# Wavelet convolution with a split-precision pyramid: level 3 in paired matmuls, up-sampling with stacked halves

## What is computed

```python
def _L1_conv_ref(x, base_w, base_b, base_scale, wconv_w, wscale):
    cur = x
    for i in range(3):                                 # three Haar levels
        co = haar2d(cur)                               # 2x2 blocks -> ll, lh, hl, hh
        cur = co[:, :, 0]
        flat = dwconv(co.reshape(B, C * 4, h, w), wconv_w[i]) * wscale[i]   # 5x5, per channel
        level_coeffs.append(flat.reshape(B, C, 4, h, w))
    next_ll = 0
    for i in reversed(range(3)):
        co = level_coeffs[i].at[:, :, 0].add(next_ll)
        next_ll = ihaar2d(co)                          # back to twice the size
    return dwconv(x, base_w) * base_scale + base_b + next_ll

x = x + _L0_conv_ref(_gn(x), ...)
x = x + _L1_conv_ref(_gn(x), ...)
```

## Time and profile before

| | us |
|---|---|
| median of 3 runs | 11311.51 (11306.57 to 11315.59) |
| the profiled execution | 11311.75 |
| its span | 11309.9 |
| PE / DVE / ACT / POOL busy | 10853.3 / 9314.2 / 6979.7 / 3419.9 |

### The profile page before, as it was taken

One profiled execution on the slowest core, in us unless ns is written; L12 is line 12 of the kernel. 1 busy time (PEld: TensorE's weight loads), 2 busy tenths in 40 slices (PEclk: granted clock), 3 DMA queues, 4 the chain that ended last, 5 costly groups with the idle time before them and its releaser, 6 DMA issues.

```text
span 11309.9 us, 208798 instructions
## 1 busy us (share of the span) xinstructions
PE 10853.3 (96%) x68772; PEld 9284.1 (82%) x68772; DVE 9314.2 (82%) x16092; ACT 6979.7 (62%) x11660; POOL 3419.9 (30%) x2756
## 2 busy tenths in 40 slices
PE   4999999999999999999599999999999999999999
PEld 4888888888888888888588888888888888888888
DVE  6989999899998989988677777777777777777777
ACT  4777777777777777788445445454454545545454
POOL 3444444344444444444222122212222122221221
PEclk9999999999999999999799999999999999999999
DMA  5333233233333333222266666666666766667665
GB/s 184 126 101 125 96 123 123 92 129 101 114 114 116 113 101 130 93 80 81 73 140 151 148 148 147 145 153 147 149 145 145 154 146 150 144 146 153 145 150 118
DMA packets 1149039, 1453.41 MB, mean 129 GB/s; under 512 B 201567, under 2 KB 1111199, under 8 KB 1111455
## 3 DMA queue, kind: packets, MB, share of 16 engines
q1 hardware_dynamic: 1147231, 1442.74, 50.1%
q10 hardware_dynamic: 1376, 6.13, 0.1%
HBM read 1040.06 MB, written 408.56 MB: 128 GB/s over the span
## 4 chain that ended last, share of the span: by engine, by line
PE 49%; DVE 1%; SPq 0%; DMA 0%; issue 0%; POOL 0%; DVEq 0%; POOLq 0%
PE ps_w L1274 10%; PE ps_w L1275 10%; PE ps_w L1276 10%; PE ps_ll L1282 4%; PE ps L1274 4%; PE ps L1275 4%; PE ps L1276 4%; PE ps_w L1317 4%; DVE ob L1399 0%; DVE x L1337 0%; DMA yb<-y_scratch 0%; SPq L1101 0%; SPq L1110 0%; DMA prm<-params 0%; SPq L1120 0%
## 5 line engine op out<-in xcount | busy, mean ns | idle before, releaser
L1274 PE MATMUL ps_w<-zb,mat 128*128 128x512 f32 x4800 | 1925.7, 401 | 1.6 <-DVE ob L1399 1.6
L1276 PE MATMUL ps_w<-zb,mat 128*128 128x512 f32 x4800 | 1907.6, 397 | 0.0
L1275 PE MATMUL ps_w<-zb,mat 128*128 128x512 f32 x4800 | 1907.2, 397 | 0.0
L1227 ACT ACTIVATE z<-x,prm 64x384 f32<-64x384 f32 (+1 forms) x3072 | 1807.2, 659 | 55.5 <-DVE x L1337 47.8
L635 POOL CAST xn_hi<-xs 96x512 fp32r<-96x512 f32 x1024 | 842.7, 823 | 3106.9 <-PE ps_qkv L660 2255.4
L1173 POOL CAST mat<-raw 128x1280 fp32r<-128x1280 f32 (+1 forms) x288 | 344.8, 1215 | 4454.8 <-DMA raw<-vec 2674.2
L1399 DVE SCALAR_TENSOR_TENSOR ob<-ps_w,prm,x 64x512 f32<-64x512 f32 x1920 | 1440.6, 750 | 148.7 <-PE ps_w L1317 109.5
L1337 DVE SCALAR_TENSOR_TENSOR x<-yb,prm,xb 128x1024 f32<-128x1024 f32 (+1 forms) x576 | 1120.4, 1997 | 421.6 <-DMA prm<-params 374.9
L658 PE MATMUL ps_qkv<-wqkv_hi,xn_hi 96*128 96x288 f32 x4096 | 1388.4, 339 | 38.0 <-POOL xn_lo L637 19.8
L637 POOL TENSOR_TENSOR xn_lo<-xs,xn_hi 96x512 fp32r<-96x512 f32 x1024 | 1363.7, 1332 | 81.9
L1247 ACT ACTIVATE ll<-ps_ll 128x512 f32<-128x512 f32 x192 | 115.1, 599 | 1880.5 <-PE ps_ll L1282 1880.5
(11 more groups left out here) (183 smaller groups left out, 24815.2 us busy)
## 6 DMA issues: line engine op xcount, KB each, us to landing
xst<-in_x SPq DMA_DIRECT2D x96, 2048.0 KB, 13.8
xs<-in_x SPq DMA_DIRECT2D x128, 1536.0 KB, 8.9
y_scratch<-ys SPq DMA_DIRECT2D x128, 1536.0 KB, 9.5
out<-ob SPq DMA_DIRECT2D x768, 208.0 KB
xb<-in_x SPq DMA_DIRECT2D x576, 256.0 KB
yb<-y_scratch SPq DMA_DIRECT2D x576, 256.0 KB
raw<-vec SPq DMA_DIRECT2D x192, 320.0 KB, 5.4
raw<-vec SPq DMA_DIRECT2D x384, 160.0 KB, 4.2
```

The source lines that it names most:

```text
L1227: last = nc.scalar.activation(z[q * WROWS:(q + 1) * WROWS, ts, b, :], x1[slot(k, g)][rows, pairs, b, q::2], ACT.Identity, scale=prm[k][row ...
L1274: mm(out_, w[HI], xx[HI], start=start, stop=False)
L1275: mm(out_, w[HI], xx[LO], start=False, stop=False)
L1276: return mm(out_, w[LO], xx[HI], start=False, stop=stop)
```

## The change

Level 3: the high and low parts of its input lie in one tile `in3_hl`, so that one matmul of 256 columns multiplies the high matrix with both; its results for high and low stand side by side in `ps_3`, and the product of the low matrix with the high input (128 columns) is added onto the first. ACT copies all of `ps_3` to `s3`, and DVE adds the two halves there (`sum3`) before `up_levels` goes on.

Up-sampling: rows 0 to 63 and 64 to 127 of `next_ll` are split apart. `next_a` holds the high part of the upper 64 rows on partitions 0 to 63 and their low part on 64 to 127; `next_b` the same for the lower rows. The matrices `up_sb` hold each half twice, one above the other, so one matmul adds high and low. Windows 0 and 1 need only the upper rows, windows 3 and 4 only the lower, window 2 both.

Of the diff only renames, sizes of tiles and the three small tensors that change their allocation are left out.

```diff
@@ ACT, steps @@
                     act.wait_ge(l3_ready, qn + 1)
-                    nc.scalar.activation(s3[:], ps_3[:, 0, 0:IMGS * HALF // 4], ACT.Copy).then_inc(s3_copied, 1)
+                    nc.scalar.activation(s3[:].rearrange("p s h n -> p (s h n)"), ps_3[:].rearrange("p s n -> p (s n)"),
+                                         ACT.Copy).then_inc(s3_copied, 1)
                     act.wait_ge(next_ready, qn + 1)
-                    nc.scalar.activation(next_p[HI][:], next_ll[:].rearrange("p n c -> p (n c)"), ACT.Copy
-                                         ).then_inc(next_hi, 1)
+                    both = next_ll[:].rearrange("p n c -> p (n c)")
+                    nc.scalar.activation(next_a[0:64, :], both[0:64], ACT.Copy).then_inc(next_hi, 1)
+                    nc.scalar.activation(next_b[64:128, :], both[64:128], ACT.Copy).then_inc(next_hi, 1)
@@ PE, steps @@
-                    level(ps_3, mat3, in3_p, HALF // 4).then_inc(l3_ready, 1)
+                    for s in range(2):
+                        for d in range(TAPS):
+                            both = (ps_3[:, s, :], mat3[HI][:, s, d, :], in3_hl[:, :, s, :, d:d + HALF // 4])
+                            high = (ps_3[:, s, 0:IMGS * HALF // 4], mat3[LO][:, s, d, :],
+                                    in3_hl[:, HI, s, :, d:d + HALF // 4])
+                            if d == TAPS - 1:
+                                mm(*high, start=False, stop=False)
+                            last = mm(*both, start=d == 0, stop=d == TAPS - 1)
+                            if d < TAPS - 1:
+                                mm(*high, start=False, stop=False)
+                    last.then_inc(l3_ready, 1)
...
                     for t in range(WINDOWS):
-                        for h in (HI, LO):
-                            last = mm(ps_w[t][:], up_sb[:, t, :], next_p[h][:], start=False, stop=h == LO)
+                        upper, lower = t < UPPER, t >= WINDOWS - LOWER
+                        if upper:
+                            last = mm(ps_w[t][:], up_sb[:, t, :], next_a[:], start=False, stop=not lower)
+                        if lower:
+                            last = mm(ps_w[t][:], up_sb[:, UPPER + t - (WINDOWS - LOWER), :], next_b[:], start=False,
+                                      stop=True)
                         last.then_inc(win_ready, 1)
@@ DVE, up_levels and split_next @@
                     dve.wait_ge(s3_copied, qn + 1)
-                    v.tensor_tensor(up3[:, :, 0], s3[:], ps_3[:, 1, 0:n], ALU.add)
-                    v.tensor_tensor(up3[:, :, 1], s3[:], ps_3[:, 1, 0:n], ALU.subtract).then_inc(up3_ready, 1)
+                    v.tensor_tensor(sum3[:], s3[:, :, 0], s3[:, :, 1], ALU.add).then_inc(s3_summed, 1)
+                    dve.wait_ge(s3_summed, qn + 1)
+                    v.tensor_tensor(up3[:, :, 0], sum3[:, 0], sum3[:, 1], ALU.add)
+                    v.tensor_tensor(up3[:, :, 1], sum3[:, 0], sum3[:, 1], ALU.subtract).then_inc(up3_ready, 1)
...
-                    dve.wait_ge(next_hi, qn + 1)
-                    v.tensor_tensor(next_p[LO][:], next_ll[:].rearrange("p n c -> p (n c)"), next_p[HI][:].bitcast(F32),
-                                    ALU.subtract).then_inc(next_lo, 1)
+                    both = next_ll[:].rearrange("p n c -> p (n c)")
+                    dve.wait_ge(next_hi, qn * 2 + 1)
+                    v.tensor_tensor(next_a[64:128, :], both[0:64], next_a[0:64, :].bitcast(F32), ALU.subtract)
+                    dve.wait_ge(next_hi, qn * 2 + 2)
+                    v.tensor_tensor(next_b[0:64, :], both[64:128], next_b[64:128, :].bitcast(F32), ALU.subtract
+                                    ).then_inc(next_lo, 1)
@@ DVE, set-up @@
-                v.tensor_copy(up_sb[:], up_raw).then_inc(down_set, 1)
+                for half, first, at in ((0, 0, 0), (64, WINDOWS - LOWER, UPPER)):
+                    n = (LOWER if half else UPPER)
+                    for to in (0, 64):
+                        v.tensor_copy(up_sb[to:to + 64, at:at + n], up_raw[half:half + 64, first:first + n]
+                                      ).then_inc(down_set, 1)
```

More of the change, by code:

```diff
@@ L95, in wt_attention_kernel @@
         mean_x, var_x, gm0, r0, nb0 = (xpar[:].rearrange("p (b t) -> p t b", t=XP)[:, t] for t in range(5))
-        same_grp = sb("same_grp", [128, 128])
-        to_grp = sb("to_grp", [128, C])
-        to_chan = sb("to_chan", [128, 3, C])
         cxy_strip = sb("cxy_strip", [C, STRIPS])
         gb = sb("gb", [C, 4])
+        until_params = ctx.enter_context(ExitStack())
+        same_grp, to_grp, to_chan = (until_params.enter_context(nc.sbuf_tensor(n, shape, F32)) for n, shape in (
+            ("same_grp", [128, 128]), ("to_grp", [128, C]), ("to_chan", [128, 3, C])))
         @dataclass
@@ L378, in _ @@
                 scales(dve, fold, 0)
-        until_params = ctx.enter_context(ExitStack())
         stat_y = until_params.enter_context(nc.sbuf_tensor("stat_y", [C, LAST * STAT], F32))
@@ L1024, in wt_attention_kernel @@
             down_sb = sbr_("down_sb", [128, WINDOWS, HALF])
-            up_sb = sbr_("up_sb", [128, WINDOWS, 2 * WROWS])
+            UPPER = -(-(HALF // 2) // (OROWS // 2))
+            LOWER = WINDOWS - HALF // OROWS
+            up_sb = sbr_("up_sb", [128, UPPER + LOWER, 2 * WROWS])
             inside_sb = sb_("inside_sb", [128, PAIRW])
@@ L1033, in wt_attention_kernel @@
             in2_p = [sbr_(f"in2_{h}", [128, 2, IMGS, HALF // 2 + 4]) for h in range(2)]
-            in3_p = [sbr_(f"in3_{h}", [128, 2, IMGS, HALF // 4 + 4]) for h in range(2)]
-            next_p = [sbr_(f"next_{h}", [128, IMGS * HALF]) for h in range(2)]
-            s3 = sb_("s3", [128, IMGS * HALF // 4])
+            in3_hl = sbr_("in3_hl", [128, 2, 2, IMGS, HALF // 4 + 4])
+            in3_p = [in3_hl[:, h] for h in range(2)]
+            next_a, next_b = (sbr_(f"next_{h}", [128, IMGS * HALF]) for h in "ab")
+            s3 = sb_("s3", [128, 2, 2, IMGS * HALF // 4])
+            sum3 = sb_("sum3", [128, 2, IMGS * HALF // 4])
             up3 = sb_("up3", [128, IMGS * HALF // 4, 2])
@@ L1056, in wt_attention_kernel @@
                 sem_(n) for n in ("l3_ready", "s3_copied", "up3_ready", "l2_ready", "low2_ready", "next_ready"))
-            win_ready = sem_("win_ready")
+            win_ready, s3_summed = sem_("win_ready"), sem_("s3_summed")
             out_ready = sem_("out_ready")
@@ L1067, in zero_pads @@
             def zero_pads(eng):
-                for t_ in (xb, yb, *zb[0], *zb[1], *in2_p, *in3_p):
+                for t_ in (xb, yb, *zb[0], *zb[1], *in2_p, in3_hl):
                     eng.memset(t_[:].bitcast(F32), 0.0).then_inc(zeroed, 1)
                 eng.memset(zero1[:], 0.0).then_inc(zeroed, 1)
-            N_ZERO = 2 + 2 * SETS + 4 + 1
+            N_ZERO = 2 + 2 * SETS + 3 + 1
             down_raw = ob[:, 0].rearrange("p b w -> p (b w)")[:, 0:WINDOWS * HALF].rearrange("p (t w) -> p t w", t=WINDOWS)
@@ L1315, in steps @@
                     for t in range(WINDOWS):
-                        for h in (HI, LO):
-                            last = mm(ps_w[t][:], up_sb[:, t, :], next_p[h][:], start=False, stop=h == LO)
+                        upper, lower = t < UPPER, t >= WINDOWS - LOWER
[4 more added lines that the diff above has]
+                                      stop=True)
                         last.then_inc(win_ready, 1)
-                pe.wait_ge(down_set, 2)
+                pe.wait_ge(down_set, 5)
                 pe.wait_ge(zeroed, N_ZERO)
@@ L1432, in _ @@
                 dve.wait_ge(mask_set, 4)
-                dve.wait_ge(down_set, 2)
+                dve.wait_ge(down_set, 5)
                 dve.wait_ge(zeroed, N_ZERO)
```

## The result

The changed kernel takes 11592.5 us (median of 4 runs, 11588.66 to 11594.73), the kernel before 11313.55 beside it: a ratio of 1.0246, interval 1.0231 to 1.0262. It is 279 us slower; 11560 was forecast, and the direction and the forecast's own range (11495 to 11615) held.

The account below looks back on a forecast made before the run. PE looked like the bound, with half a microsecond per group before DVE with POOL (A) or the DMA queue (B) set the pace. 95 pairs x (2.47 + 0.17) = 251 us on 11311.75 gave 11560, range 11495 to 11615.

Parts of the forecast that it names:

- slack of half a microsecond: Second half: what PE can give per group before DVE with POOL, or the DMA queue, set the pace.
- the sum for PE alone: Second half: fewer level-3 and up-sampling matmuls would shorten a group by 1.19 us on PE alone.
- A: Second-half group where POOL builds level-2 and level-3 matrices; its turns with DVE make it 31.93 us, 2.47 more.
- F: Start of DVE's first finish (L1399), for window 0, in a second-half group; group lengths count from it to the next.
- B: Second-half group where SP loads the next channel's matrices and parameters; set by the DMA queue, 29.7 us, 0.17 more.
- rival 4: PE idles 3.8 us in A, its clock falls, about 4 us at half rate lose 2 us: 11620; chance 0.10.
- (a): DVE's new addition of two SBUF operands, 256 columns, ahead of up_levels: 0.45 us with its wait.
- (b): DVE's split_next becomes two instructions on 64 partitions: 0.69 us becomes about 1.30; ACT's copy also becomes two.
- Rival 1: In A, POOL leaves DVE the same work behind it as before: A 30.01 us, time 11380; chance 0.18.
- Rival 2: In A, POOL's casts pass without holding DVE: A 1.0 us less, time 11230; chance 0.12.
- Rival 3: PE's whole gain arrives in the second half because both side chains shrink with it: 11085; chance 0.04.
- (c): ACT copies 512 columns of level 3 instead of 128: costs nothing.

Follow-up runs that it names:

- e1: Changed kernel with POOL building only the first 4 of 128 columns of the level-2 and level-3 matrices: 11080.65 us (ratio 0.9794).
- e5: Changed kernel with level 3's sums through PSUM, so that up_levels reads at most one SBUF operand per instruction: 11332.59 us (ratio 1.0019).
- e4: Changed kernel with twelve more, unused matmuls filling PE's idle time at the end of each group A: 11544.01 us (ratio 1.0205).
- e11: e9 plus make_x1 moved ahead of trailing in group A and between trailing and up_levels in group B: 11072.82 us (ratio 0.9787).
- e3: Changed kernel with only the up-sampling half of the change, level 3 and up_levels as before: 11344.79 us (ratio 1.0029).
- e9: Changed kernel with both edits of e5 and e6, sums through PSUM and parameters loaded first: 11167.69 us (ratio 0.9873).
- e2: Changed kernel with only the level-3 half of the change, up-sampling and splitting as before: 11508.58 us (ratio 1.0171).
- e7: e6 plus DVE doing make_x1 ahead of trailing in group A: 11392.17 us (ratio 1.0073).
- e6: Changed kernel with the parameters loaded ahead of the ten loads of raw matrices in SP's order: 11563.74 us (ratio 1.0221).
- e8: Kernel before the change with parameters loaded first and make_x1 ahead of trailing in group A: 11311.14 us (ratio 1.0000).
- e10: Changed kernel with both edits of e4 and e6, PE filled in group A and parameters loaded first: 11423.88 us (ratio 1.0098).
- e12: e11 without the sums through PSUM, so up_levels reads two SBUF operands as in the changed kernel: 11154.70 us (ratio 0.9862).

## Why the prediction was right

*Bound and slack.* That the other loops and not PE decide is borne out from both sides: with POOL's work gone (e1) the same matmuls run at 28.3 us a group, 1.2 less than before, as the sum for PE alone had it; with it in place nothing of that arrives. The slack of half a microsecond itself was read from the waits; no run gains just that much. Level 3 takes 2.38 us in the trace where 2.34 was worked out:

```profile
8031.56 0.28 PE L1319 MATMUL ps<-in_hl,mat 128*128 128x256 f32 x1
...
8033.94 0.28 PE L1279 MATMUL ps<-in,mat 128*128 128x256 f32 x1
```

*A.* The forecast walk and the trace, from F: third L1353 (now L1372) to its end 17.05 and 17.04, the second L1350 18.78 and 18.69, the new addition 21.85 and 21.75, start of the last stretch in effect (the end of the first up3 24.77 and 24.68), end of the second split 28.28 and 28.28, next F 31.93 and 31.91. Each turn was where it was put, to 0.10 us. Two things carried it: that a waiting cast gets in between two queued DVE instructions, and that up_levels had come to read two SBUF operands. Before the runs only the earlier trace rows spoke for the second, where up_levels with one operand in PSUM runs beside the casts at 0.29 us; e5 shows it by itself (first up3 0.29 us, in the changed kernel 2.90); the first is in the rows above (the second cast 1.71 us, L1369 beside it 1.73). e4's eleven groups show what the moment of the first cast is worth: 1.5 us later, and A is 1.9 us shorter.

*B.* Here the size was off, 29.7 against 30.04, 0.34 x 95 = 32 us and all of the difference between 11560 and the measurement. The queue was rightly read (e4: 29.76 with the clock full in B). What failed is the weight given to rival 4: I gave the clock one chance in ten and put nothing for it into B. The idle time was foretold, 3.8 us (3.46 in the trace), and the clock fell after every one of these pauses. B is thus the later of two ends in each group, the queue's and PE's, and its mean lies above both: in the groups where the clock stayed low for the usual time DVE hardly waited for PE at the next F (0.03 us), in the 13 where it stayed low for twice as long it waited 1.05 us. Rival 4's 4 us at half rate are in the trace of the kernel before, right after PE's idle time of 69.75 us: ten matmuls from 5634.02 to 5638.42, 0.44 us from one to the next, with a granted clock of 0.50 from 5634 to 5638 and of 1.00 from 5639 to 5650. In the changed kernel it is 3.41 us after 81 of the 94 pauses and 6.83 after 13. That rival's own number, 11620, took 2 us for a fall where the usual one costs 1.5, and was too high by about as much (28 us) as the forecast was too low (33). One slip of arithmetic stands in the range: its terms (0.2 for B, 0.3 for (a) and (b)) put the upper end at 11610, not 11615; nothing hangs on it.

*The rivals.* Rival 1 did not hold in the changed kernel. Its condition, casts that come too late for `trailing`, is met in eleven groups of e4, and A is 30.0 us there. Rival 2 (casts run free) is excluded by L1372's 1.75 us. Rival 3 has its number, 11085, in e11's 11073, once both side chains had been shortened by hand; the change alone did not do it.

*(a), (b), (c).* The splits cost their 0.69 each and ACT's wider copy nothing; e1, with all of them in, runs at PE's pace.

## What to carry to other kernels

Before taking work off a busy engine, find for each repeated stretch how long every *other* loop takes from its start to the same point of the next; the smallest slack bounds what the edit can bring (here 0.5 us of 1.2, by the waits). An edit that makes one engine's signal come earlier moves whoever listens to it: look which instructions of other engines its own then run beside (here POOL's casts went from F + 16.07 to F + 15.06, into `trailing`). And trading a PSUM operand for one in SBUF was not free on DVE with POOL at work beside it: the first up3 instruction took 2.90 us in the changed kernel and 0.29 in e5.

## What the runs showed of the hardware that I had not expected

*What stood before each fall of the clock.* This table counts, over the traces of all fourteen kernels and in their second half (5710 us to 60 us before the end), the pauses in PE's work of 0.7 us and more. Every one of the 354 falls of the granted clock there comes with a pause, during it or at most 1.6 us after PE starts again. The last column has the traces, as pauses and, after the slash, falls:

| pause of PE, us | pauses | with a fall of the clock | pauses / falls by trace |
|---|---|---|---|
| 0.7 to 1.6 | 388 | 0 | e3 179 / 0, e9 93 / 0, e5 62 / 0, changed 23 / 0, e2 21 / 0, e4 9 / 0, e7 1 / 0 |
| 1.6 to 1.9 | 77 | 7 | e4 33 / 1, e7 24 / 5, e5 16 / 1, e1, e2, e3, e9 1 / 0 each |
| 1.9 to 2.4 | 149 | 63 | e5 69 / 29, e4 37 / 7, e7 33 / 23, e2 7 / 3, e3 3 / 1 |
| 2.4 to 3.3 | 136 | 95 | e2 88 / 66, e7 37 / 22, e4 5 / 3, e5 5 / 4, changed 1 / 0 |
| 3.3 to 3.6 | 189 | 189 | changed 94 / 94, e6 94 / 94, e5 1 / 1 |

The kernel before, e8, e10, e11 and e12 have no such pause there, and a granted clock of 1.00 over the whole stretch; the changed kernel has 0.97 (5710 to 11529), e2 0.98. The shortest pause with a fall is 1.77 us (e7, PE starts again at 11015.93; granted clock 0.50 from 11016.5 to 11019), the longest without one 3.15 us (e2, PE starts again at 5793.29; 1.00 from 5788 to 5800). The slow stretch does not begin at a fixed point: after the pauses of 3.46 to 3.56 us of the changed kernel the granted clock falls anywhere from 1.0 us before PE starts again to 1.3 us after it (in the rows above, 8056.32 and 8057.68, it is among the latest). A slow stretch is 3.41 us long in 331 of the 354 falls and 6.83 in the other 23 (13 in the changed kernel, 7 in e6, 3 in e7): seven or eight matmuls at 0.43 us, in some groups about fourteen, and then the full clock.

*Turns between DVE and POOL.* In the group A above POOL's second cast (1.25 us by itself) was issued at 8039.30, while the third L1372 ran until 8039.90 and L1369 came next; it ended at 8041.01, and L1369, issued at 8039.82, at 8041.55. So the cast did not wait for DVE's queue to drain: it got in after the instruction that ran. The two subtractions (2.92 us each by themselves) did the same: they took 6.20 us together from 8041.20, with L1396 and L1398 beside them at 3.13 and 2.90. POOL's 8.4 us of work went by almost without loss to POOL (done at F + 24.5, was 25.4), and most of its length, 7.36 us, fell on DVE.
